# Cross-attention's last iteration carries each finished chunk on to residual, moments and router logits

## What is computed

```python
x1 = layernorm(x + attn(x))
slots = x1
for _ in range(3):
    q      = rmsnorm(slots) @ Wq.T
    attn   = softmax over slots, normalised over context
    slots  = gru_cell(attn @ v_proj, slots, ...)      # r, z, n gates
x2 = layernorm(x1 + slots)
logits = x2 @ router_w + router_b + expert_bias       # 8 experts
probs = softmax(logits); top 2, renormalised
out = layernorm(x2 + sum of gate * expert(x2))
```

## Time and profile before

| what | value |
| --- | --- |
| time, median of 3 (lowest, highest) | 1310.94 us (1310.27, 1312.8) |
| the profiled execution's own time | 1308.93 us |
| its span | 1307.0 us |
| mean granted TensorE clock | 0.943 |
| busy: TensorE, weight load | 1183.5 us (91%), 991.7 us (76%) |
| busy: VectorE, ScalarE, GpSimd | 904.8 us (69%), 715.2 us (55%), 247.4 us (19%) |

### The profile page before, as it was taken

How to read it: one execution, slowest core, us unless ns; L and a number is a source line. 1 busy time by engine, 2 the same in 40 slices (tenths; PEclk the granted TensorE clock), 3 DMA queues, 4 the chain that set the end, 5 groups by cost and what they waited for, 6 DMA issues and landing times. The chain is left out here.

```text
span 1307.0 us, 19549 instructions
## 1 busy us (share of the span) xinstructions
PE 1183.5 (91%) x6246; PEld 991.7 (76%) x6246; DVE 904.8 (69%) x2044; ACT 715.2 (55%) x1260; POOL 247.4 (19%) x277
## 2 busy tenths in 40 slices
PE   4889897699999999999999999999646999999991
PEld 2567676578777887877878787788546999999991
DVE  4654645787765678776567777654666888888884
ACT  3435546376673327667333866733323777767772
POOL 2110110000000000000000000000003767777761
PEclk9799898899999999999999999999756999999996
DMA  8201001000001000000100000060690223222224
GB/s 271 77 1 49 17 4 30 25 1 1 1 1 33 9 17 1 1 1 1 33 9 17 1 1 1 1 258 33 202 282 26 42 40 48 40 44 44 44 32 141
DMA packets 49848, 61.42 MB, mean 47 GB/s; under 512 B 9201, under 2 KB 41395, under 8 KB 49651
## 3 DMA queue, kind: packets, MB, share of 16 engines
q1 hardware_dynamic: 40196, 48.44, 11.4%
q0 software_dynamic: 8832, 12.11, 5.9%
...
## 5 line engine op out<-in xcount | busy, mean ns | idle before, releaser
L77 PE MATMUL x_psum<-x_s_lo,x_kq_hi 128*128 128x512 f32 (+1 forms) x312 | 126.4, 405 | 12.4 <-PEq L246 8.7
L77 PE MATMUL x_psum<-x_p_lo,x_v_hi 128*128 128x512 f32 (+1 forms) x312 | 124.4, 399 | 0.0
L78 PE MATMUL x_psum<-x_s_hi,x_kq_lo 128*128 128x512 f32 (+1 forms) x312 | 123.9, 397 | 0.0
L79 PE MATMUL x_psum<-x_s_hi,x_kq_hi 128*128 128x512 f32 (+1 forms) x312 | 123.7, 397 | 0.0
L79 PE MATMUL x_psum<-x_p_hi,x_v_hi 128*128 128x512 f32 (+1 forms) x312 | 123.3, 395 | 0.0
L78 PE MATMUL x_psum<-x_p_hi,x_v_lo 128*128 128x512 f32 (+1 forms) x312 | 123.3, 395 | 0.0
L1062 POOL TENSOR_TENSOR x_sq<-x_sq 128x512 f32<-128x512 f32 x12 | 15.5, 1293 | 562.8 <-ACT x_sq L1048 562.8
L1212 DVE CUSTOM_DVE_ANT_0 x_e<-x_psum,x_rsb,x_rs 128x512 f32<-128x512 f32 (+1 forms) x117 | 86.4, 747 | 50.0 <-PE x_psum L79 49.0
L77 PE MATMUL e_bank<-e_w_lo,e_g_hi 128*128 128x256 f32 x368 | 108.1, 294 | 0.1
L77 PE MATMUL e_bank<-e_xT_lo,e_w_hi 128*128 128x256 f32 x368 | 105.7, 287 | 1.4 <-DVE e_xT_lo L1963 1.4
L79 PE MATMUL e_bank<-e_xT_hi,e_w_hi 128*128 128x256 f32 x368 | 105.3, 286 | 0.0
...
## 6 DMA issues: line engine op xcount, KB each, us to landing
...
h_w<-in_mlp_w SPq DMA_DIRECT2D x2, 1024.0 KB, 10.5
...
```

What stands on the lines that cost most here:

```text
L77: pe.matmul(out, w_hi, x_lo, start=start, stop=False)
L78: pe.matmul(out, w_lo, x_hi, start=False, stop=False)
L79: return pe.matmul(out, w_hi, x_hi, start=False, stop=stop)
```

## The change

The work of `route` up to the logits moves into earlier places, and the logits are computed another way:

- Since x2 = rs * (x1 + s) + nb with nb = -mean * rs, the logits are rs * (x1 @ W + s @ W) + nb * (column sums of W) + biases. No normalised row has to be turned back.
- x1 @ W (`raw_logits`) is done in the head from `sT` while it still holds x1: 8 matmuls of 8 columns per chunk on TensorE, for chunks 0 and 1 in the border behind the square sums, for chunks 2 and 3 at the head's end. With the first go two more, for the column sums. VectorE copies them out (`take_logits`); those of chunks 2 and 3 stand behind all `slots_lo`.
- In the last iteration TensorE does `turn_rows(c)` (8 transposes, 8 matmuls of 8 columns) for chunk 0, 1, 2 inside half (1,1), (2,0), (3,0), between `gate(3)` and `gate(4)`, and for chunk 3 behind the last gate. Behind the argument of the tanh and ahead of the state update VectorE does `add_rows(0)`, `(1)`, `(2)` in (1,1), (2,1), (3,0) and `logits(0)`, `(1)`, `(2)` in (2,0), (3,0), (3,1); both for chunk 3 at the end. ScalarE does `apply(0)` in (2,1), `apply(1)` in (3,1), `apply(2)` behind the gates.
- SP: x1's four loads go out ahead of w1, the stores of chunks 0 to 2 follow w1, and SP waits for them before the block ends. `route` keeps b1, b2, w2, the stores of chunk 3 and the gate rows; ScalarE applies chunk 3 there, behind the exponential. The router's weights are loaded in the head.

Cut to its core:

```diff
             load_x(2)
+            sp.dma_start(first["rout_w"][:], io["router_w"].rearrange("(c p) e -> p c e", p=P)).then_inc(first["ld_rout"], 16)
+            sp.dma_start(first["rout_b"][:, 0], io["router_b"].partition_broadcast(P)).then_inc(first["ld_rout"], 16)
+            sp.dma_start(first["rout_b"][:, 1], io["expert_bias"].partition_broadcast(P)).then_inc(first["ld_rout"], 16)
...
+            def take_logits(c):
+                v.wait_ge(first["raw_mm"], c + 1)
+                if c == 0:
+                    v.tensor_copy(first["rout_sum"][:], bank[7][:, TPC * NE:(TPC + 1) * NE])
+                v.tensor_copy(first["lg"][:, c * TPC:(c + 1) * TPC], bank[7][:, 0:TPC * NE].rearrange("p (t e) -> p t e", e=NE)).then_inc(first["raw_ok"], 1)
...
                     turned_lo(a)
                     if c >= 1:
                         first["rms"](v, k, 0, c - 1)
+                        take_logits(c - 1)
...
                     for cc in range(1, LAST):
                         for h in range(DH):
                             first["slots_lo"](v, 0, cc, h)
-                    v.wait_ge(vchain, k.base + k.n)
+                    take_logits(LAST - 1)
+                    take_logits(LAST)
...
+            def raw_logits(c):
+
+                pe.wait_ge(x1_sb, DH * (c + 1))
+                pe.wait_ge(z_ok, DH * min(c + 2, NC))
+                if c == 0:
+                    pe.wait_ge(first["ld_rout"], 48)
+                    for h in range(DH):
+                        pe.matmul(bank[7][:, TPC * NE:(TPC + 1) * NE], ones[:], first["rout_w"][:, h], start=(h == 0), stop=(h == DH - 1))
+                if c == LAST:
+                    pe.wait_ge(first["raw_ok"], LAST)
+                for j in range(TPC):
+                    for h in range(DH):
+                        last = pe.matmul(bank[7][:, j * NE:(j + 1) * NE], sT[:, h, tok(c, j)], first["rout_w"][:, h],
+                                         start=(h == 0), stop=(h == DH - 1))
+                last.then_inc(first["raw_mm"], 1)
...
                     first["square_sums"](pe, 0, c - 1)
+                    raw_logits(c - 1)
...
             turn_x1(LAST)
+            raw_logits(LAST - 1)
+            raw_logits(LAST)
...
+            def apply(c):
+                act.wait_ge(norm_ok, c + 1)
+                for j in range(TPC):
+                    t = c * TPC + j
+                    act.activation(x2_rows[c][:, j], x2_rows[c][:, j], ACT.Identity, bias=c_nb[:, t:t + 1], scale=c_rs[:, t:t + 1]).then_inc(x2_ok, 1)
+
...
+            def add_rows(c):
+
+                v.wait_ge(x1_back[c], 16)
+                for i in range(DH):
+                    v.wait_ge(turn_mm, c * DH + i + 1)
+                    v.tensor_tensor(x2_rows[c][:, 2 * i:2 * i + 2], bank[6 + i].rearrange("p (t d) -> p t d", d=D),
+                                    x2_rows[c][:, 2 * i:2 * i + 2], ALU.add).then_inc(added, 1)
+                v.wait_ge(added, DH * (c + 1))
+                for j in range(TPC):
+                    k.mark(v.bn_stats(c_stats[:, j], x2_rows[c][:, j]))
+                v.wait_ge(vchain, k.base + k.n)
+                for j in range(TPC):
+                    k.mark(v.bn_aggr(c_mv[:, j], c_stats[:, j]))
+                v.wait_ge(vchain, k.base + k.n)
+
+            def logits(c):
+
+                ts = tiles_of(c)
+                k.step(v.tensor_scalar(c_nb[:, ts], c_mv[:, :, 1], EPS_LN, None, ALU.add))
+                rsqrt_steps(v, k, c_rs[:, ts], c_nb[:, ts], c_tmp[:])
+                v.wait_ge(logit_mm, c + 1)
+                k.mark(v.tensor_tensor(lg[:, ts], bank[0][:, c * TPC * NE:(c + 1) * TPC * NE].rearrange("p (t e) -> p t e", e=NE), lg[:, ts], ALU.add))
+                k.step(v.scalar_tensor_tensor(out=c_nb[:, ts], in0=c_mv[:, :, 0], scalar=-1.0, in1=c_rs[:, ts], op0=ALU.mult, op1=ALU.mult))
+                v.sem_inc(norm_ok, 1)
+                k.mark(v.tensor_tensor(lg[:, ts], lg[:, ts], bc(c_rs[:, ts], 2, NE), ALU.mult))
+                k.step(v.tensor_tensor(part[:], bc(c_nb[:, ts], 2, NE), bc(rout_sum[:], 1, TPC), ALU.mult))
+                k.step(v.tensor_tensor(part[:], part[:], bc(rout_b[:, 0], 1, TPC), ALU.add))
+                k.step(v.tensor_tensor(lg[:, ts], lg[:, ts], part[:], ALU.add))
...
                         if h == 0 and c + 2 < NC:
                             normed(c + 2)
+                        if not more and (c, h) in ((2, 0), (3, 0), (3, 1)):
+                            logits(c + h - 2)
+                        if not more and (c, h) in ((1, 1), (2, 1), (3, 0)):
+                            add_rows(c - 1)
                         v.wait_ge(n_ok, i + 1)
...
+            add_rows(LAST)
+            logits(LAST)
...
+            sp.wait_ge(acc_ok, ITERS * MT * 2)
+            sp.wait_ge(p_lo_ok, (ITERS - 1) * NP + MT * KEEP)
+            x1 = io["x1"].rearrange("(t p) d -> p t d", p=P)
+            for c in range(NC):
+                sp.dma_start(x2_rows[c][:], x1[:, tiles_of(c)]).then_inc(x1_back[c], 16)
             sp.wait_ge(upd_mm, ITERS * NP)
             sp.wait_ge(row_mm, ITERS)
             for ex in range(NE):
                 if ex == NE - 1:
                     sp.wait_ge(mult_ok, ITERS * NC)
                 sp.dma_start(w1[:, ex], io["w1"][ex].rearrange("(c p) f -> p c f", p=P)).then_inc(shared["ld_e"], 16)
+            rows, totals = (io[n][0:T].rearrange("(t p) d -> p t d", p=P) for n in ("x2", "totals"))
+            for c in range(LAST):
+                sp.wait_ge(x2_ok, TPC * (c + 1))
+                sp.dma_start(rows[:, tiles_of(c), 0:D], x2_rows[c][:]).then_inc(kept, 16)
+                sp.dma_start(totals[:, tiles_of(c)], x2_rows[c][:]).then_inc(kept, 16)
+            sp.wait_ge(kept, 16 * 2 * LAST)
...
+                def turn_rows(c):
+                    pe.wait_ge(s_ok, it * GH + (c + 1) * DH)
+                    pe.wait_ge(mult_ok, (it + 1) * NC)
+                    if c >= 1:
+                        pe.wait_ge(added, c * DH)
+                    tok = [slice((c * TPC + j) * P, (c * TPC + j + 1) * P) for j in range(TPC)]
+                    for j in range(TPC):
+                        for h in range(DH):
+                            last = pe.transpose(bank[6 + j // 2][:, (j % 2) * D + h * P:(j % 2) * D + (h + 1) * P], sT[:, h, tok[j]], ident[:])
+                        if j % 2 == 1:
+                            last.then_inc(turn_mm, 1)
+                    for j in range(TPC):
+                        for h in range(DH):
+                            last = pe.matmul(bank[0][:, (c * TPC + j) * NE:(c * TPC + j + 1) * NE], sT[:, h, tok[j]], rout_w[:, h],
+                                             start=(h == 0), stop=(h == DH - 1))
+                    last.then_inc(logit_mm, 1)
...
                         if c >= 1 and h == 1 and it + 1 < ITERS:
                             square_sums(pe, it + 1, c - 1)
+                        if it + 1 == ITERS and (c, h) in ((1, 1), (2, 0), (3, 0)):
+                            turn_rows(c - 1)
                         if i > 0:
                             pe.wait_ge(arg_ok, it * GH + i)
                         gate(4, 2, h, c, "u", in_mm)
                         if i > 0:
                             pe.wait_ge(z_ok, it * GH + i)
                         gate(5, 1, h, c, "su", z_mm)
+                if it + 1 == ITERS:
+                    turn_rows(LAST)
...
         @block.sync
         def _(sp):
-            x1 = io["x1"].rearrange("(t p) d -> p t d", p=P)
-            for c in range(NC):
-                ts = slice(c * TPC, (c + 1) * TPC)
-                sp.dma_start(x2[:, ts], x1[:, ts]).then_inc(loaded[c], 16)
-            sp.dma_start(rw[:], io["router_w"].rearrange("(c p) e -> p c e", p=P)).then_inc(ld_r, 16)
-            sp.dma_start(rb[:, 0], io["router_b"].partition_broadcast(P)).then_inc(ld_r, 16)
-            sp.dma_start(rb[:, 1], io["expert_bias"].partition_broadcast(P)).then_inc(ld_r, 16)
-
             sp.dma_start(b1[:], io["b1_cols"]).then_inc(ld_e, 16)
             sp.dma_start(b2[:], io["b2"].rearrange("e d -> (e d)").partition_broadcast(P)).then_inc(ld_e, 16)
             for e in range(NE):
                 sp.dma_start(w2[:, e], io["w2"][e].rearrange("(c p) f -> p c f", p=P)).then_inc(ld_e, 16)
 
-            rows = io["x2"].rearrange("(t p) d -> p t d", p=P)
-            sp.wait_ge(x2_ok, NT)
-            sp.dma_start(rows[:, :, 0:D], x2[:]).then_inc(kept, 16)
-            sp.dma_start(io["totals"][0:T].rearrange("(t p) d -> p t d", p=P), x2[:]).then_inc(kept, 16)
+            rows, totals = (io[n][0:T].rearrange("(t p) d -> p t d", p=P) for n in ("x2", "totals"))
+            sp.wait_ge(x2_ok, TPC)
+            sp.dma_start(rows[:, NT - TPC:, 0:D], x2[:]).then_inc(kept, 16)
+            sp.dma_start(totals[:, NT - TPC:], x2[:]).then_inc(kept, 16)
             sp.wait_ge(gates_ok, TOP)
             sp.dma_start(rows[:, :, D:], gate_rows[:]).then_inc(kept, 16)
```

(8 more changed lines are left out.)

123 lines of the change are left out of this document (38 added, 85 removed).

## The result

| what | before | after |
| --- | --- | --- |
| time, median (lowest, highest; runs) | 1310.97 us (1310.27, 1312.8; 5) | 1305.47 us (1303.94, 1305.99; 5) |
| profiled execution, its span | 1308.93, 1307.0 us | 1305.99, 1304.3 us |
| mean granted TensorE clock | 0.943 | 0.946 |
| busy: TensorE, VectorE, ScalarE | 1183.5, 904.8, 715.2 us | 1178.8, 903.4, 708.9 us |

The ratio is 0.9953, with a 95% interval of 0.9938 to 0.9969: the change made the kernel 5.5 us faster. Forecast was 1311.6, no change, in a range of 1305.0 to 1317.5. The time lies inside the range, 0.5 us above its lower end, but it moved clearly, and the forecast said that it would not.

What follows compares the result with a forecast made beforehand. The gap between last gate and experts was taken as the routing block, 62.5 us: 35.8 logits, 26.7 decision. Terms: -35.8 + 7.6 + 13.1 + 8.2 + 7.6 = +0.7 us, median 1311.6, range 1305.0 to 1317.5.

Steps and rivals of the forecast that it cites:

- Part 1: Routing block: its logit part is removed, -35.8 us.
- part 2: Remaining routing block: ends on SP's queue of 10.5 MB at 34.3 us, more than VectorE's 27.6; 28.2 us shorter than before.
- The rival that the queue is quicker: Routing block: SP's queue beats w2's row, 410 GB/s as for w1; -4.4 us, to 1307.2; within the faster chance, 0.28.
- Part 3: Last iteration's gates: last state 13.1 us later, 8.1 from TensorE's added work and 5.0 from VectorE's queue.
- Part 4: Last chunk's work behind the gates, covered by nothing: +8.2 us, the block starting 8.5 after the last state.
- Part 5: Head: x1 logits at half clock, +3.3 us in the first border and +4.3 at the head's end, 7.6 together.
- The other half of part 5: Head's end: logits of chunk 3 behind all `slots_lo`, at half clock, with all engines waiting: +4.3 us.
- the faster one: Routing block's queue quicker than w2's row: 1307.2 us, or 1304.4 with the head at 0.5 too; chance 0.28.
- The slower one: Last gates: TensorE's clock falls in `turn_rows`, 2.6 us each for (0), (1), 1.4 for (2); 1315.6 to 1318.2; chance 0.32.

Runs made afterwards that it cites:

- e_route: Changed kernel with the routing block's SP queue reordered: last chunk's stores and gate rows ahead of most of w2, same bytes; 1307.57 us, 0.9977.
- e_rate: Changed kernel with w2 loaded in rows of 8 KB instead of 1 KB and w1's copies reading with a step of 8 values; 1342.37 us, 1.0244.
- e_all: Changed kernel with chunk 3's x1 logits right behind chunk 2's, e_gates' order, stores ahead of most w2 loads and w2 on its own semaphore; 1299.11 us, 0.9914.
- e_all2: e_all with the two copies of x1 logits moved ahead of the last six slots_lo; 1299.12 us, 0.9912.
- e_gates: Changed kernel with VectorE's carried work in the last gates reordered: logits(0), (1) earlier, add_rows behind the state update; 1304.7 us, 0.9954.

## Why the prediction was right and wrong

- **Part 1, the block removed, and part 2, what is left of it:** right. 34.6 us against 34.3, on the queue, at 347 GB/s, and VectorE's chain 27.7 us against 27.6. `e_route` and `e_rate` show that it was the queue. The rival that the queue is quicker is wrong for this kernel, and right about its cause: rows of 8 KB would have made it so. Its price was too high: 4.4 us for 410 GB/s, where `e_rate` at 423 gave a block 2.4 to 3.1 us shorter. One sum in part 2 is off: at 435 GB/s the part's 24 us and its own 4.3 us of start and end make 28.4, above VectorE's 27.6, so the queue would still have set the end; the prediction's 449 GB/s is the right figure for that.
- **Part 3, the gates:** right, +12.7 against +13.1; TensorE's share 7.8 against 8.1, the rest 4.9 against 5.0, with the wait at `turn_rows(2)` where it was put.
- **Part 4, the tail:** right, 8.67 us from the last state to the block against 8.5.
- **Part 5, the step that failed:** it priced `raw_logits(0)` with the clock that the kernel before had in that border, "the granted clock is 0.50", so "20 x 0.215 = 4.3 us", and from it "The projection then starts at 153.4 instead of 149.89, its second half 3 us later, and the next `up` follows it without pause: **+3.3**". In both profiles of the changed kernel the clock there was 1.00. The matmuls took 2.15 us, the projection's first half 2.11 instead of 4.18, and its second half waited 2.15 us for ScalarE's copy: it starts 43.1 us behind x1 turned with and without the logits. The cost was 0.0; the +0.5 that the part gives for full clock was too much as well, since that wait is longer at full clock (2.61 us without the logits) than the 0.62 of before. Where the clock was 0.50 (`e_all`, `e_all2`, `e_rate`) the cost was 0.75, 0.76 and 2.4 us: of the prediction's order only where the clock stayed low through the projection's first half, and less where it came back sooner. The part held a clock of one border of one trace for a property of the place. The other half of part 5, +4.3 at the head's end, was right.
- **A term that was left out:** -1.3 us from the first score to iteration 3's gates. Some of it is the clock at the first scores, which is back 4.0 us after they begin (at 258.4) instead of 5.3; but in the second profile of before it is back after 3.8. It is no gain of the change that I could show: that second profile has 614.88 us in this stage, and `e_gates`, with the changed kernel's program here, 614.98, against 614.24 and 614.14 of the changed kernel. What sets the moment stays open.
- **The sum:** with 4.3 - 1.3 for the head and what follows it instead of 7.6, and -0.4, +0.2 and -0.2 from the later stages, the forecast of +0.7 becomes -4.3. The experts' -0.6, which is within what two profiles of one kernel differ by (308.5 and 309.3 from the first matmul on), makes it -4.9, the first pair's difference without its first stage; the mean of both pairs is -4.5.
- **The rivals:** the faster one gave the right time by the wrong mechanism. 1304.4 was the queue's rate with a cheap head; it was the head, with the unforeseen -1.3, and the queue kept w2's rate. That the time lies in the range is luck in part, as its low end was made up of the same two terms. The slower one, the clock's fall in `turn_rows`, did not come in the two profiles of the changed kernel, came once in `e_gates`, and costs 1.0 there instead of the 1.4 to 2.6 that I had for each.
- **What a measurement tells:** single times of one kernel lie up to 9 us apart, so that the profiled pair's 2.9 us and the runs' 5.5 us are no contradiction. I had taken the first three runs, 2.5 us apart, for the spread.
- **What stays open:** how often the clock is full in the first border of the changed kernel. Two profiles had it so; the other nine with logits there had it so six times.
